# Where the small jobs of an attention pipeline stand: behind the transposes and passes, drained behind the exponentials

## The reference

```
# layer 0, a non-local block without softmax
theta, phi, g = conv1x1(x) each (64 channels, with bias)
pairwise = theta^T phi / 1024          (1024 x 1024)
z = x + out_conv(pairwise g)
# layer 1, attention over pixels
scores = theta(z)^T phi(z) / sqrt(128) (1024 x 1024)
attn   = softmax(scores, rows)
out    = z + conv1(attn z)
```

## Time and profile before

| | us |
|---|---|
| median of 3 runs (lowest to highest) | 177.67 (177.56 to 177.97) |
| profiled execution, its own time | 177.83 |
| its span, first to last instruction | 175.9 |
| busy: PE, DVE, ACT, POOL | 164.4, 131.7, 94.5, 56.9 |
| the 32 exponentials (line 521), one | 1.117 |
| the 32 row maxima (line 667), one | 1.224 |
| the 32 row shifts (line 810), one | 0.625 mean, 0.367 least, 0.372 median, 0.926 most |

### The profile page before, as it was taken

One profiled execution on the slowest core, in us unless ns is written; L12 is line 12 of the kernel. 1 busy time (PEld: TensorE's weight loads), 2 busy tenths in 40 slices (PEclk: granted clock), 3 DMA queues, 4 the chain that ended last, 5 costly groups with the idle time before them and its releaser, 6 DMA issues.

```text
span 175.9 us, 2602 instructions
## 1 busy us (share of the span) xinstructions
PE 164.4 (93%) x967; PEld 136.1 (77%) x967; DVE 131.7 (75%) x217; ACT 94.5 (54%) x178; POOL 56.9 (32%) x73
## 2 busy tenths in 40 slices
PE   7989887999899999999899999999898999998994
PEld 6968675777678888888687887888687888886893
DVE  1316689997897998577699999775699889899512
ACT  3023647786645752577454754547546665666410
POOL 1015021716400081404603073401623042733120
PEclk9999999999999999999999999999999999999999
DMA  4603000030000010000001010000001001000111
GB/s 136 193 0 123 0 0 0 0 121 4 2 0 0 4 60 0 0 0 4 0 0 60 0 49 16 0 0 0 4 0 60 3 0 63 0 0 0 60 60 63
DMA packets 2829, 4.76 MB, mean 27 GB/s; under 512 B 448, under 2 KB 1280, under 8 KB 2816
## 3 DMA queue, kind: packets, MB, share of 16 engines
q1 hardware_dynamic: 2304, 4.39, 7.2%
q10 hardware_dynamic: 512, 0.20, 0.6%
HBM read 2.49 MB, written 2.10 MB: 26 GB/s over the span
## 4 chain that ended last, share of the span: by engine, by line
PE 75%; DVE 18%; ACT 3%; DMA 2%; issue 1%; ACTq 0%
PE numer L336 22%; PE turned L317 9%; PE ring L222 8%; DVE negmax L667 7%; PE ring L224 7%; PE ring L223 7%; PE aux L281 4%; PE aux L222 2%; PE aux L343 2%; DVE PT_lo L682 2%; DMA pg_w<-pg_weights_dram 2%; PE aux L228 2%; PE ring L228 2%; DVE P L675 2%; DVE t_lo L643 2%; PE aux L234 2%
## 5 line engine op out<-in xcount | busy, mean ns | idle before, releaser
L667 DVE TENSOR_REDUCE negmax<-ring 128x1 f32<-128x1024 f32 x32 | 39.2, 1224 | 18.4 <-PE ring L224 17.9
L810 POOL TENSOR_SCALAR shift<-negmax,rho 128x1 f32<-128x1 f32 x32 | 20.0, 625 | 94.3 <-DVE negmax L667 83.5
L521 ACT ACTIVATE P<-ring,shift 128x1024 f32<-128x1024 f32 x32 | 35.8, 1117 | 9.8 <-POOL shift L810 9.6
L682 DVE TENSOR_TENSOR PT_lo<-turned,PT_hi 128x512 fp32r<-128x512 f32 x62 | 40.4, 682 | 0.4 <-ACT PT_hi L529 0.4
L529 ACT ACTIVATE PT_hi<-turned 128x512 fp32r<-128x512 f32 x62 | 33.7, 595 | 10.0 <-PE turned L317 10.0
L317 PE MATMUL turned<-identity,P 128*128 128x128 f32 x256 | 33.8, 274 | 1.8 <-DVE PT_lo L682 1.8
L317 PEld LDWEIGHTS turned<-identity,P 128*128 128x128 f32 x256 | 29.3, 141 | 5.6 <-DVE P L675 2.3
L675 DVE TENSOR_SCALAR P<-P,rden 128x1024 f32<-128x1024 f32 x32 | 29.8, 933 | 1.1
L222 PE MATMUL ring<-Z_hi,t_hi 128*128 128x512 f32 x64 | 25.6, 400 | 0.6 <-DVE t_lo L712 0.6
L223 PE MATMUL ring<-Z_hi,t_lo 128*128 128x512 f32 x64 | 25.2, 393 | 0.0
L224 PE MATMUL ring<-Z_lo,t_hi 128*128 128x512 f32 x64 | 25.1, 393 | 0.0
(11 more groups left out here) (116 smaller groups left out, 201.2 us busy)
## 6 DMA issues: line engine op xcount, KB each, us to landing
out_dram<-result SPq DMA_DIRECT2D x7, 256.0 KB, 2.1
X<-x_dram SPq DMA_DIRECT2D x3, 512.0 KB, 3.5
X<-x_dram SPq DMA_DIRECT2D x2, 256.0 KB, 4.1
out_dram<-result SPq DMA_DIRECT2D x1, 192.0 KB, 1.9
w<-weights_dram SPq DMA_DIRECT2D x1, 128.0 KB, 5.2
wi<-inner_dram ACTq DMA_DIRECT2D x1, 64.2 KB, 5.4
pg_w<-pg_weights_dram ACTq DMA_DIRECT2D x1, 64.0 KB, 3.5
pg_b<-pg_bias_dram ACTq DMA_DIRECT2D x1, 64.0 KB, 5.1
```

The source lines that it names most:

```text
L521: nc.scalar.activation(P[:, n % P_BUFFERS, :], ring[:, n % 2, :], ACT.Exp, bias=shift[:, t:t + 1], accum_out=den[:, t:t + 1]).then_inc(pro ...
L667: nc.vector.tensor_reduce(negmax[:, t:t + 1], ring[:, n % 2, :], AX.X, ALU.max, negate=True).then_inc(max_ready, 1)
L682: nc.vector.tensor_tensor(PT_lo[:, group % GROUPS, half_chunks(half), rows], turned[:, columns(half)].rearrange("p (j r) -> p j r", j=CHUN ...
L810: nc.gpsimd.tensor_scalar(shift[:, t:t + 1], negmax[:, t:t + 1], rho[:, b % 2, t:t + 1], rho[:, b % 2, t:t + 1], ALU.subtract, ALU.add).th ...
```

## The change

The diff below moves calls and alters no computation. On PE the first job goes behind the transposes, ahead of the attention piece; the second job goes behind the attention piece. Every job stands one step earlier: pg0 and pg1 in t = 0, MT and R in t = 1, A and Z0 in t = 2, Z1 in t = 3, t0 and V0 in t = 4, V1 and V2 in t = 5, t1 in t = 6. On ACT the first job is drained behind exps(n+2), the second job at the start of the next step. On DVE the low half of the first job comes behind both low_turned, that of the second job at the start of the next step, ahead of row_max. On POOL low_x and split_z stand one step earlier.

```diff
@@ PE; in both helpers each job's t is one less (pg: t == 0 and b > 1)
             for n in range(ALL - 1):
                 b, t = divmod(n, TILES)
                 if n + 2 < ALL:
                     scores(n + 2)
-                if b + 1 < IMAGES:
-                    early_job(b + 1, t)
                 turn(n, 0)
                 turn(n, 1)
                 if b + 1 < IMAGES:
-                    late_job(b + 1, t)
+                    early_job(b + 1, t)
                 if n >= GT:
                     attend(n // GT - 1, n % GT)
+                if b + 1 < IMAGES:
+                    late_job(b + 1, t)
@@ ACT; the helpers' t as on PE
             for n in range(ALL - 1):
                 b, t = divmod(n, TILES)
+                if t and b + 1 < IMAGES:
+                    late_job(b + 1, t - 1)
                 if n >= 2 * GT and n % GT == 0:
                     copy_numer(n // GT - 2)
+                high_turned(n, 0)
+                high_turned(n, 1)
+                if n + 2 < ALL:
+                    exps(n + 2)
                 if b + 1 < IMAGES:
                     early_job(b + 1, t)
-                high_turned(n, 0)
-                high_turned(n, 1)
-                if b + 1 < IMAGES:
-                    late_job(b + 1, t)
-                if n + 2 < ALL:
-                    exps(n + 2)
@@ DVE; the helpers' t as on PE
             for n in range(ALL - 1):
                 b, t = divmod(n, TILES)
+                if t and b + 1 < IMAGES:
+                    late_job(b + 1, t - 1)
                 if n + 2 < ALL:
                     row_max(n + 2)
+                norm(n + 1)
+                low_turned(n, 0)
+                low_turned(n, 1)
                 if b + 1 < IMAGES:
                     early_job(b + 1, t)
-                norm(n + 1)
-                low_turned(n, 0)
-                if b + 1 < IMAGES:
-                    late_job(b + 1, t)
-                low_turned(n, 1)
@@ POOL
                     if t == 0:
                         high_x(i + 1)
+                        low_x(i + 1, 0)
                     if t == 1:
-                        low_x(i + 1, 0)
-                    if t == 2:
                         low_x(i + 1, 1)
+                    if t == 3:
+                        split_z(i + 1, 0)
                     if t == 4:
-                        split_z(i + 1, 0)
-                    if t == 5:
                         split_z(i + 1, 1)
```

More of the change, by code:

```diff
@@ L408, in early_job @@
                     first_value_part()
-                if t == 1 and b > 1:
+                if t == 0 and b > 1:
                     job_pg(b, 0)
+                if t == 1:
+                    job_MT(b)
                 if t == 2:
-                    job_MT(b)
+                    job_A(b)
                 if t == 3:
-                    job_A(b)
+                    job_Z(b, 1)
                 if t == 4:
-                    job_Z(b, 1)
+                    job_t(b, 0)
                 if t == 5:
-                    job_t(b, 0)
+                    job_V(b, 1)
                 if t == 6:
-                    job_V(b, 1)
-                if t == 7:
                     job_t(b, 1)
@@ L426, in late_job @@
                     job_V(0, 2)
-                if t == 1 and b > 1:
+                if t == 0 and b > 1:
                     job_pg(b, 1)
+                if t == 1:
+                    job_R(b)
                 if t == 2:
-                    job_R(b)
-                if t == 3:
                     job_Z(b, 0)
+                if t == 4:
+                    job_V(b, 0)
                 if t == 5:
-                    job_V(b, 0)
-                if t == 6:
                     job_V(b, 2)
@@ L574, in early_job @@
                     first_v_high(1)
+                if t == 1:
+                    copy_MT(b)
                 if t == 2:
-                    copy_MT(b)
+                    high_A(b)
                 if t == 3:
-                    high_A(b)
+                    make_Z(b, 1)
                 if t == 4:
-                    make_Z(b, 1)
+                    high_t(b, 0)
                 if t == 5:
-                    high_t(b, 0)
+                    high_V(b, 1)
                 if t == 6:
-                    high_V(b, 1)
-                if t == 7:
                     high_t(b, 1)
@@ L590, in late_job @@
                     high_V(0, 2)
+                if t == 1:
+                    copy_R(b)
                 if t == 2:
-                    copy_R(b)
-                if t == 3:
                     make_Z(b, 0)
+                if t == 4:
+                    high_V(b, 0)
                 if t == 5:
-                    high_V(b, 0)
-                if t == 6:
                     high_V(b, 2)
@@ L743, in early_job @@
                     first_v_low(1)
-                if t == 1 and b > 1:
+                if t == 0 and b > 1:
                     make_pg(b, 0)
-                if t == 3:
+                if t == 2:
                     low_A(b)
+                if t == 4:
+                    low_t(b, 0)
                 if t == 5:
-                    low_t(b, 0)
+                    low_V(b, 1)
                 if t == 6:
-                    low_V(b, 1)
-                if t == 7:
                     low_t(b, 1)
@@ L757, in late_job @@
                     low_V(0, 2)
-                if t == 1 and b > 1:
+                if t == 0 and b > 1:
                     make_pg(b, 1)
+                if t == 4:
+                    low_V(b, 0)
                 if t == 5:
-                    low_V(b, 0)
-                if t == 6:
                     low_V(b, 2)
```

## The result

| | before | after |
|---|---|---|
| median of 4 runs (lowest to highest), us | 177.62 (177.28 to 177.97) | 198.24 (196.81 to 199.56) |
| ratio, 95% interval | | 1.116 (1.113 to 1.120) |
| profiled execution: time, span | 177.83, 175.9 | 198.37, 196.6 |
| mean granted clock of the profiled execution | 1.000 | 0.965 |

The change made the kernel 20.6 us slower. I had forecast 193.3, with 186.5 to 197.0 as the range: the direction and most of the size came, but the time lies above the range.

A forecast was written before the change was run, and what follows sets the result against it. PE's own instruction order was taken as the bound (busy 93% of the span). Adding +7.0 us for steps 0 to 7 and +8.6 for two images to 177.83 gave 193.4, as a median 193.3; range 186.5 to 197.

The forecast's parts named there:

- The drain of the first job at +5.0: On ACT, behind exps(n+2): the first job's drain starts 5.01 us after the first matmul of scores(n+2).
- the long shift: POOL's row shift starting together with DVE's scaling of P: 0.91 us instead of 0.37, in every pair step.
- the wait on aux: On PE, the second job waits for the first's drain from the single aux bank, stalling from about +4.4.
- the serial chain per step: Each step costed by its chain, 3.67 to 7.23 us; 45.13 us per image of jobs against 40.84.
- (3) The stall is there but the granted clock falls with it: PE at half clock, 2.1 us in each of 15 pairs: up to 31 more, 225; a few, 200 to 210; chance 0.04.
- copy_numer and the late row maximum: copy_numer stays ahead of high_turned on ACT; t1's low part delays one DVE row maximum by 0.5 us; costed at nothing.
- a last image that changes its length: Sign of being wrong: the last image, from 139.91, has no jobs and was to keep its length.
- my sum of hops: Chain from scores through row maximum and shift to exponentials at +3.92 us, with ACT free at +5.01.
- (1), the shift that isn't blocked: POOL's shift starts ahead of the scaling, exponentials 0.54 us earlier in twelve pairs: 6.5 us less, 186.8; chance 0.12.
- (2), faster: The attention piece between two jobs, 1.4 us of cover, closes PE's gaps: 6.1 us idle goes, 171.7; chance 0.02.

The follow-up runs named there:

- the warm kernel: The changed kernel with idle bf16 matmuls of 128 columns added in PE's stalls; 194.25 us against 198.24.
- the sixth experiment: The kernel before with only PE's new order and the earlier steps, ACT and DVE draining at the places of before; 178.73 us, ratio 1.005.

## Why the prediction was wrong

**The mechanism was right.** The drain of the first job at +5.0, the long shift (0.90 to 0.93 us in 29 of 32 cases, 15 before), the wait on aux and the serial chain per step came as written: 45.5 us an image for 45.13, 43.5 us for steps 0 to 7 at full clock (21.61 to 65.14 in the warm kernel) for 43.5. The warm kernel measures the whole sum at the granted clock that I assumed: 194.25 against 193.3. That the loss is the drains' place was shown from three sides: by 173.34 us with the first job's drain put right and all else as changed, by 178.73 with all drains put back, and by 230.64 with PE's order put back in their stead, which makes it worse.

**The step that failed** is in the rivals, "(3) The stall is there but the granted clock falls with it", and what I made of it, "0.04", and in the range, which left it out. The rows of before showed a clock of 1.00 and no stall anywhere near 2 us. They said nothing against a fall, and I read their silence as evidence. The price I gave it was for all 15 pairs (31 us), or 200 to 210 for "a few of them". What happened is smaller: in the profiled run the clock fell three times, twice between steps 1 and 3 (2.9 us together) and once in step 21 (1.2 us), together the 4 us that the warm kernel takes back. A pair step lost 1.2 or 1.3 us by it (8.06 for 6.83, 7.91 for 6.65), where I had priced 2.1. Without these 4 us the time is inside the range. Of the four runs three had a mean clock of 0.965 and one 0.982; the latter was the fastest, 196.81. The rule of the Trainium skill that I quoted, "TensorE: Matmul & The Clock Gate", section "Part 1: The HAM clock gate (the "warmup" mystery)", that an idle PE has its clock halved, agrees with this trace as far as it goes: the clock falls to 0.50 inside the 2.42 us stall of step 1, and it is 1.00 again in step 4. It also falls behind some of the shorter stalls and not behind others, see the last section.

**Two small terms.** I costed copy_numer and the late row maximum at nothing, "without that room it would be 0.5 per image", and I had named a last image that changes its length as a sign of being wrong. It does change: 18.78 us for 18.33 in steps 24 to 28. The row maximum of step 23 starts at +2.14, behind t1's low half, its exponentials end late, and copy_numer of step 24 stands behind them. In step 24, without a job to stand between, the room isn't there. ACT's drain of numer and the piece of attention that waits for it:

```profile
162.03 0.68 ACT L539 ACTIVATE attended<-numer,bias 128x512 f32<-128x512 f32 x1
...
162.76 0.50 PE L336 MATMUL numer<-PT_hi,V_hi 128*128 128x512 f32 x1 [0.18 <-ACT attended L539]
```

It ends 0.05 us ahead of PE's piece; the step lasts 4.13, 0.47 over 3.67. In steps 8 and 16, pg0 covers it. And the chains by way of the exponentials are 0.08 to 0.13 longer than my sum of hops, 0.4 per image with the jobs' single steps. In the profiled runs the warm kernel has 194.56 where I had 193.4, 1.16 us more, and these two terms make 1.3; between the medians it is 0.95.

**The other rivals.** (1), the shift that isn't blocked, did not come; made to come, it gave the 0.54 per chain that I had priced, but the same lock moved to the scaling beside POOL's longer work (1.59 us for 0.75). The Trainium skill, "SBUF — State Buffer", section "SBUF: two separate sides", which I had weighed, says just this, that the one who starts first holds the ports and the other blocks, and the trace agrees with 1.59. I had worked out only the half that gains. (2), faster, wanted ACT's drain of the first job from +2.9: with it at +3.16 the kernel runs in 173.34, near the 171.7 that I had given that case. I had the number for the better kernel in the list of rivals and took it only as unlikely, which for this change it was.

## What to carry to other kernels

When a job is moved behind other work on its own engine, follow its drain too: the cover is the time from the job's end to the next user of its buffer, and a drain behind a long chain (maximum, shift, exponential) spends it all. If the forecast says that PE will stall 2 us at a time, give the lowered clock a term and a share of the range, even where the trace of before never shows it; a trace without stalls can't speak against it. And an instruction moved away from a shared port meets something else there: look at what.

## What the runs showed of the hardware that I had not expected

The clock does not fall at every stall of a length. Steps 4, 12 and 20 each have PE idle for 2.1 us in one piece: behind the first two the clock stays at 1.00, behind the third it falls to 0.50 at 144.0. The 1.64 us of step 2 were followed by a fall at 41.6, the 1.78 us of steps 5 and 13 by none. The stall alone doesn't decide; what does was not settled, and the runs of one kernel differ (0.965 and 0.982 here; 1.00 and 0.99 in the sixth experiment). Idle matmuls in two thirds of the stalls held the mean clock at 1.00 in all four runs and took the spread of the runs from 2.75 us to 0.6.
